# A two-layer LoRA kernel: the start in another order, B0's transposes behind the first two steps, and W1 and C' moved by tiles of columns

## The reference

```
x = x + (x W0^T + b0 + (x A0[id0]^T) B0[id0]^T)          # 32 adapters of rank 16
x = x + (x W1^T + b1 + 2 * (x A1[id1]) B1[id1])          # 32 slots of rank 16
return x
```

## Time and profile before

| | before |
|---|---|
| median of three runs | 2145.63 us |
| the profiled execution | 2145.09 us, of which the span is 2143.3 us |
| TensorE busy in matmuls | 2077.1 us (97%) |
| VectorE busy | 1594.9 us (74%) |
| ScalarE / GpSimd busy | 737.2 us (34%) / 708.3 us (33%) |
| moved by DMA | 459.08 MB, mean 214 GB/s |
| granted TensorE clock, mean of the span | 0.994 |

### The profile page before, as it was taken

One profiled execution on the slowest core, in us unless ns is written; L12 is line 12 of the kernel. 1 busy time (PEld: TensorE's weight loads), 2 busy tenths in 40 slices (PEclk: granted clock), 3 DMA queues, 4 the chain that ended last, 5 costly groups with the idle time before them and its releaser, 6 DMA issues.

```text
span 2143.3 us, 27962 instructions
## 1 busy us (share of the span) xinstructions
PE 2077.1 (97%) x9388; PEld 1715.2 (80%) x9388; DVE 1594.9 (74%) x2177; ACT 737.2 (34%) x1298; POOL 708.3 (33%) x506
## 2 busy tenths in 40 slices
PE   4999899999999999999999999999999999999999
PEld 4887687778788878888887888888888887888887
DVE  3677767967776887687877686877776886777876
ACT  4663223233322323333333333333333333333332
POOL 1133303444121545041444140544130544221443
PEclk9999999999999999999999999999999999999999
DMA  9895838796755798564798564789574688564676
GB/s 233 261 337 156 246 113 235 214 299 205 213 165 163 213 280 271 151 203 140 214 284 292 147 222 125 212 270 314 150 221 118 214 261 303 158 218 123 210 217 197
DMA packets 322298, 459.08 MB, mean 214 GB/s; under 512 B 28012, under 2 KB 135532, under 8 KB 321644
## 3 DMA queue, kind: packets, MB, share of 16 engines
q1 hardware_dynamic: 255084, 334.59, 50.9%
q10 hardware_dynamic: 67072, 122.71, 19.1%
HBM read 383.80 MB, written 74.45 MB: 214 GB/s over the span
## 4 chain that ended last, share of the span: by engine, by line
PE 76%; DVE 12%; DMA 5%; issue 3%; SPq 2%; ACT 1%; ACTq 0%; POOL 0%; DVEq 0%
PE acc L1436 22%; PE acc L1438 22%; PE acc L1437 22%; DVE w_lo L990 4%; DVE c_acc L1096 2%; PE h_acc L1366 2%; PE h_acc L1362 2%; DVE xop_lo L1015 2%; DVE c_out L1166 2%; DVE x_sum L1005 2%; PE acc L1376 1%; DMA b_raw<-pb_t 1%; DMA w_raw<-v_t 1%; PE acc L1321 1%; PE acc L1306 1%
## 5 line engine op out<-in xcount | busy, mean ns | idle before, releaser
L1436 PE MATMUL acc<-xop_hi,w_hi 128*128 128x512 f32 x2688 | 1061.0, 395 | 34.4 <-DVE w_lo L990 30.3
L791 POOL TENSOR_TENSOR w_raw<-w_raw,w_second 128x512 f32<-128x512 f32 x464 | 655.6, 1415 | 1272.0 <-DMA w_second<-wc_t 504.8
L1437 PE MATMUL acc<-xop_hi,w_lo 128*128 128x512 f32 x2688 | 1050.4, 391 | 0.0
L1438 PE MATMUL acc<-xop_lo,w_hi 128*128 128x512 f32 x2688 | 1050.1, 391 | 0.0
L990 DVE TENSOR_TENSOR w_lo<-w_raw,w_hi 128x512 fp32r<-128x512 f32 x672 | 595.9, 890 | 386.5 <-ACT w_hi L828 383.0
L828 ACT ACTIVATE w_hi<-w_raw 128x512 fp32r<-128x512 f32 x672 | 424.0, 631 | 1169.7 <-PE acc L1438 976.7
L1436 PEld LDWEIGHTS acc<-xop_hi,w_hi 128*128 128x128 f32 x2688 | 506.9, 189 | 153.5 <-DVE w_lo L990 46.9
L1438 PEld LDWEIGHTS acc<-xop_lo,w_hi 128*128 128x128 f32 x2688 | 507.1, 189 | 106.7
L1437 PEld LDWEIGHTS acc<-xop_hi,w_lo 128*128 128x128 f32 x2688 | 507.3, 189 | 101.6
L1005 DVE TENSOR_TENSOR x_sum<-x_in 128x512 f32<-128x512 f32 x240 | 222.6, 939 | 0.1
L1166 DVE TENSOR_TENSOR c_out<-acc,c_out 128x512 f32<-128x512 f32 x304 | 201.9, 681 | 7.8 <-PE acc L1376 6.2
(11 more groups left out here) (90 smaller groups left out, 890.6 us busy)
## 6 DMA issues: line engine op xcount, KB each, us to landing
w_raw<-wc_t SPq DMA_DIRECT2D x448, 256.0 KB, 3.9
w_second<-wc_t ACTq DMA_DIRECT2D x320, 256.0 KB, 4.4
w_raw<-v_t SPq DMA_DIRECT2D x208, 256.0 KB, 4.0
w_second<-v_t ACTq DMA_DIRECT2D x144, 256.0 KB, 4.4
x_in<-x_t SPq DMA_DIRECT2D x128, 256.0 KB, 6.3
out_t<-c_out SPq DMA_DIRECT2D x128, 256.0 KB, 5.3
w_part<-w_t SPq DMA_DIRECT2D x32, 512.0 KB, 6.8
x_in<-w_t SPq DMA_DIRECT2D x64, 256.0 KB, 6.1
```

The lines of the kernel that those rows point to most:

```text
L791: nc.gpsimd.tensor_tensor(w_raw[:, r, :], w_raw[:, r, :], w_second[:, n % RAW2, :], ALU.add if sign > 0 else ALU.subtract).then_inc(w_summ ...
L1436: nc.tensor.matmul(bank[:, :], wh, xh, start=(k == 0), stop=False)
L1437: nc.tensor.matmul(bank[:, :], wl, xh, start=False, stop=False)
L1438: mm = nc.tensor.matmul(bank[:, :], wh, xl, start=False, stop=end)
```

## The change

It has five parts.

1. *Layout of U.* A new view `x_pre` lies over `x_in`: tiles by column block first. A load takes 512 neighbouring floats (2 KB) of one row block for each partition and fills one column block of four moving tiles. There are still eight loads a block, of 256 KB each. Readers see a tile as 4 pieces of 128 floats, 4 KB apart.
2. *Layout of C'.* A view `c_pre` does the same for C', but for blocks 0 and 1 of pass 0. Two tiles are stored by one DMA, in rows of 1 KB: the 64 stores of 256 KB become 16 of 256 KB and 24 of 512 KB.
3. *Loads at the start.* ScalarE's queue issues A1 and SyncE's B0; before it was the other way round. Parts 4 and 5 are loaded ahead of the biases. B1's rows are loaded in the first two steps, and the store of `b0t_t` stands in step 2.
4. *Copies and splits at the start.* VectorE copies parts 0 and 1 out of PSUM. ScalarE and VectorE split the first two weights and parts 0 and 1 before they turn to U's tiles; A1 is split ahead of step 0. `h_bias` is zeroed by ScalarE.
5. *B0's transposes.* They stand behind steps 0 and 1 (`B_AFTER`), eight each, and what hangs on them one to two steps later.

The diff, cut to its core:

```diff
-    E_AFTER, Q_AFTER = 3, (5, 6)
+    B_AFTER, E_AFTER, Q_AFTER = (0, 1), 3, (5, 6)
...
+        x_pre = over("x_pre", [P, 4, TT, KH, P], fp32, "x_in")
+        c_pre = over("c_pre", [P, 4, TT, KH, P], fp32, "c_out")
...
+        def by_columns(pl, b):
+            return pl < PRE and (pl, b // 2) != (0, 0)
...
             def load_x(pl, half, th, k):
                 b = block_no(half, th)
                 if pl < PRE:
-                    sp.dma_start(as_tiles(x_in[:, b, k, :]), columns_of(w1_t, pl, th, half * KH + k)
-                                 ).then_inc(x_loaded[b], 16)
+                    o, kh = divmod(k, 2)
+                    row = (half * KH + kh * KS) * P
+                    sp.dma_start(flat(x_pre[:, b, o, kh * KS:(kh + 1) * KS, :]),
+                                 w1_t[(2 * pl + th) * TT + o, :, row:row + SW]).then_inc(x_loaded[b], 16)
...
                         if pl < PRE:
+                            if by_columns(pl, b) and m % 2 == 0:
+                                continue
...
+                            if by_columns(pl, b):
+                                src = c_pre[:, b, :, m - 1:m + 1, :].rearrange("p o m n -> p o (m n)")
+                                row -= P
...
             for b in range(BATCH):
-                sp.dma_start(a1_raw[:, b, :, :], lora_a1[...]).then_inc(a1_loaded, 16)
+                sp.dma_start(b0_rows[b * RANK:(b + 1) * RANK, :], lora_b0[...]).then_inc(b0_loaded, 16)
+            for n in PARTS_AT[-1]:
+                load_part(n + PIN)
             for l, bias_d in enumerate((bias0, bias1)):
                 sp.dma_start(bias[:, l, :], bias_d).then_inc(bias_loaded, 16)
...
+                if g < 2:
+                    for b in range(4 * g, 4 * g + 4):
+                        sp.dma_start(b1_rows[b * RANK:(b + 1) * RANK, :], lora_b1[...]).then_inc(b1_loaded, 16)
+                if g == 2:
+                    sp.wait_ge(t_copied, 4)
+                    sp.dma_start(b0t_t[:, :], flat(b0t_raw[:, :, :])).then_inc(b0t_stored, 16)
...
             # TensorE, in the loop of steps
+                    if s in B_AFTER:
+                        pe.wait_ge(b0_loaded, BATCH * 16)
+                        for n in range(2 * s, 2 * s + 2):
+                            turn(n, [b0_rows[:, (4 * n + i) * P:(4 * n + i + 1) * P] for i in range(4)])
```

More of the change, by code:

```diff
@@ L197, in parts_split @@
     def parts_split(g):
-        return [n for n in range(NPART) if PART_G_AT[n] == g + 1]
+        return [n for n in range(2, NPART) if PART_G_AT[n] == g + 1]
     def ended(n):
@@ L392, in block_no, with as_tiles, shaped, x_of @@
             return half * 2 + th
+        def as_tiles(ap):
+            return ap.rearrange("p (o n) -> p o n", o=TT)
+        def shaped(pl, ap):
+            return as_tiles(ap) if pl < PRE else ap
+        def x_of(pl, b, k):
+            return x_pre[:, b, :, k, :] if pl < PRE else x_in[:, b, k, :]
+        def by_columns(pl, b):
+            return pl < PRE and (pl, b // 2) != (0, 0)
+        def c_of(pl, b, m):
+            return c_pre[:, b, :, m, :] if by_columns(pl, b) else shaped(pl, c_out[:, b, m, :])
         def x_tile(q, which, k):
             dh, th = PRODUCTS[q % NPROD][3][which]
-            return x_in[:, block_no(dh, th), k, :]
+            return x_of(q // NPROD, block_no(dh, th), k)
+        def stores(b, pl):
+            return sum(MH // 2 if by_columns(p, b) else MH for p in range(pl))
         def wait_x(eng, q, which):
@@ L537, in load_w @@
                     for b in range(4):
-                        sp.wait_ge(out_stored[b], (PRE if i == M2 else 1) * MH * 16)
+                        sp.wait_ge(out_stored[b], stores(b, PRE if i == M2 else 1) * 16)
                 sp.wait_ge(w_lo_ready, s - RAW + 1)
@@ L657, in _ @@
             for n in PARTS_AT[-1]:
-                load_part(n + PIN)
-            for n in PARTS_AT[-1]:
                 store_part(n)
-            for b in range(BATCH):
-                sp.dma_start(b1_rows[b * RANK:(b + 1) * RANK, :],
-                             lora_b1[bass.ds(adapter_of(1, b), 1), :, :].rearrange("o r n -> (o r) n")
-                             ).then_inc(b1_loaded, 16)
-            sp.wait_ge(t_copied, 4)
-            sp.dma_start(b0t_t[:, :], flat(b0t_raw[:, :, :])).then_inc(b0t_stored, 16)
             for g in range(NG):
@@ L894, in load_second @@
                     for b in range(4):
-                        act_e.wait_ge(out_stored[b], (PRE if i == M2 else 1) * MH * 16)
+                        act_e.wait_ge(out_stored[b], stores(b, PRE if i == M2 else 1) * 16)
                 if n >= RAW2:
@@ L1189, in _ @@
                     w_split_lo(g + 2)
-                if g == 0:
-                    dve.wait_ge(a1_hi_ready, 1)
-                    nc.vector.tensor_tensor(a1_lo[:, :, :, :], a1_raw[:, :, :, :].rearrange("p b k r -> p k b r"),
-                                            f(a1_hi[:, :, :, :]), ALU.subtract).then_inc(a1_lo_ready, 1)
                 for n in parts_split(g):
                     split_part_lo(n)
-                if g == 0:
+                if g - 1 in B_AFTER:
+                    for n in range(2 * (g - 1), 2 * g):
+                        t_copy(n, flat(b0t_raw[:, 4 * n:4 * n + 4, :]))
+                if g == 2:
                     dve.wait_ge(t_copied, 4)
```

115 lines of the change are left out of this document (62 added, 53 removed).

## The result

| | before | after |
|---|---|---|
| median of five runs each, same chip | 2145.63 us (2140.78 to 2146.95) | 2128.48 us (2124.88 to 2136.15) |
| ratio, with its 95% interval | | 0.993 (0.9905 to 0.9955) |
| the profiled execution | 2145.09 us | 2124.88 us, of which the span is 2123.2 |

A forecast was written before the change was run, and what follows sets the result against it. TensorE, busy 97% of the span, was taken as the bound, gains coming only from idle time and low clock. Start 17.8, M3 6.0 and later waits 4.0 make 27.8 us off 2145.09: 2117 us, range 2105 to 2131.

The forecast's parts named there:

- two rivals (2126 and 2127): Supply gives out behind the start, 2126 us, chance 0.15; only the start's gain comes, 2127 us, chance 0.12.
- the start alone: Rival, chance 0.12: `q_half`'s round trips keep their own latency, later stalls stay, only the start's 17.8 us come: 2127 us.
- the start: Up to the small matmuls ahead of step 2: reached at 33.1 us, not 50.88; 17.8 us won, bounds 13.2 and 20.0.
- the stall in M3: M3 of pass 0: stall of 8.8 us behind U's loads shrinks; 6.0 us won, between 0 and 8.8.
- the signs that I had named for "right": Early first matmul, no `vp_lo` wait, small matmuls at full clock, U's window over 300 GB/s, short M3 wait and load issues.
- the signs for "wrong": U after 20 us, waits for parts in steps 2 to 5, 5 us wait ending M3, or VectorE lines 50 ns dearer.
- The premise of the start: In 7.5 to 20 us, U's 512-byte pieces cost about double: 174 GB/s, against 309 to 349 with longer rows.
- The second rival: Rival, chance 0.09: 512 bytes cost nothing, the queues' mix is slow; U lands at 23.2, 11.1 us won, 2134 us.
- the small matmuls: The 24 ahead of step 1 run without a wait at the high clock, 3.02 us, where they took 5.04.
- 350 to 850 us: TensorE's 16.4 us of waits in 13 places: a quarter, 4.0 us, won; between 8 won and 2 lost.
- The supply: Rival, chance 0.15: 13.1 MB in the first 44 us come late, TensorE waits in steps 2 to 5, 9 us lost: 2126.
- The pieces: Rival, chance 0.04: reading or writing in pieces slows VectorE in passes 0 and 1; at 0.3 us each, 2153 us.

The follow-up runs named there:

- E1: Changed kernel with U loaded in pieces of 512 bytes again, against the changed kernel: 2133.43 us, ratio 0.9952 to the kernel before.
- E9: Changed kernel with U's loads and C's stores as in the kernel before, so the new order alone: 2131.97 us, ratio 0.9936 to the kernel before.
- E3: Kernel before with the new layouts of U and C' and nothing else: 2141.55 us, ratio 0.9979 to the kernel before.
- E6: Changed kernel with A1 and B0 swapped back to the queues they had before: 2134.67 us in one run.
- E7: Kernel before with each load of B0's rows going to 16 partitions eight apart, not 16 neighbours: 2140.37 us, ratio 0.998 to the kernel before.
- E4: Changed kernel with B0's first eight transposes put behind the small matmuls ahead of step 1: 2126.87 us, ratio 0.9934 to the kernel before.
- E11: Changed kernel again, unedited, for a second profile: 2129.95 us, ratio 0.9931 to the kernel before.
- E2: Changed kernel with C' stored as before, 64 stores of 256 KB in pieces of 512 bytes: 2126.82 us, ratio 0.9918 to the kernel before.
- E10: Changed kernel with each load of B0's rows cut into four column pieces of 2 KB rows, still to 16 neighbouring partitions: 2133.51 us in one run.

## Why the prediction was right, and where it was not

The time, 2128.48 us, lies in the range only because two rivals (2126 and 2127) had pulled its upper end over my forecast's own range. The gain, 15 to 17 us, is a little over half of the 27.8 us that I had summed, and the nearest number on my list is that of the rival "the start alone", 2127. Its account is not what happened: the start won less than it said, and the stall in M3 did shrink. Of the signs that I had named for "right", four failed: the first 128x512 matmul starts at 19.17 (16 to 19 said), the small matmuls ahead of step 2 at 36.79 (near 33), the wait in M3 ends at 222.47 and is 3.79 us (near 215 and under 2), and SyncE takes 3.31 us for the first two of U's loads there (well under 1 us each). None of the signs for "wrong" showed in the profile after.

- **The premise of the start failed.** I wrote "So the pieces of 512 bytes cost about double". E1 and E9 move the same pieces at 318 to 320 GB/s, and E3 moves rows of 2 KB at 192. What made the window slow were B0's rows beside U: moved to ScalarE's queue again they bring 209 GB/s back (E6), spread over the partitions they let 272 through (E7). The result was on my side because the change did both things at once, which is luck. The second rival had the mechanism (the mix of the queues), and a wrong time: it let U land at 23.2 as before, though the change takes B0 out of the mix.
- The Trainium skill, page "DMA: Bandwidth & Descriptors", section "Specifications", gives 512 bytes as the least transfer for line rate. The runs agree: 318 to 320 GB/s in pieces of 512 bytes, 340 in rows of 2 KB (windows of 7.5 to 20 us, with rows of 1 KB among them). I had weighed that rule and gave it 0.09, on the ground that "the share is full and the bytes are few"; a full share says that packets are under way, not that they are short or long.
- **The start was mis-sized: 17.8 said, 14.1 measured at the place I named (50.88 minus 36.79), 13.2 kept (11.3 to 13.8 over four profiles).** The rate of U was right (340 GB/s, U at 15.87). The difference is in B0's rows again: part 2 shares its time with them and lands 1.1 us late, TensorE waits 2.2 us for them at 25.5 (I had them at 22.1, at 330 GB/s; the window moved 156), and step 0 itself takes 7.06 us in place of 6.47. That last 0.6 us is the clock: matmuls start 0.42 us or more apart for the first 5.0 us of step 0 (to 23.4), for 3.7 us in the kernel before (to 32.4), and the 1.3 us more at half the pace cost about 0.65 by estimate. That is 3.9 us; the rest of the chain up to there was 0.2 faster than I had it. Behind step 3 `make_e` waits 0.8 us for `b0t_lo`, which I had costed at nothing. In E4, without the wait for B0, TensorE waits 1.9 us for a copy of ScalarE's.
- What I said of the small matmuls was right in the first profile: no wait for `vp_lo`, a clock of 1.00, 24 in 2.95 us ahead of step 1. In E11 and E2 the clock fell there behind the wait for B0 (4.45 and 4.44 us). I had priced B0's lateness at its own length.
- **M3: 6.0 said, 3.7 in the first profile, 1.5 as the mean over the profiles.** The sum itself was off: 3.52 us and a third of the remaining 5.3 are 5.3 us, not 6.0. I had said that nearly all of the stall hangs on U's backlog, and let the matmuls at the slow clock go with it. A wait of 2.9 us or more stays in every profile, the matmuls behind it still run slowly (the first takes 0.80 us after as before), and in five kernels a second wait followed.
- **350 to 850 us: 4.0 said, nothing measured.** TensorE waits 15.9 us in 12 places there after (330 to 830) against 16.4 in 13; the 4th to 14th product took 529.6 to 538.6 us in all kernels, in no order. "A quarter" stood on no row. The waits of TensorE from 330 to 830 us:

```profile
PE acc L1474 <- DVE w_lo L1021: 15.9, 12, 3.2
```

- The supply held (in steps 2 to 5 TensorE waits for no part). The pieces cost VectorE nothing: 997 ns for `scale_c` against 987, 877 for `xop_lo` against 928, 888 for the sums against 912 and 680 for the updates against 679. The 928 holds eight instructions of pass 2 that the changed kernel has in a row of their own at 1091 ns; without them, at that price, it would be about 887. Groups by form on VectorE to 850 us, after:

```profile
L1036 DVE TENSOR_TENSOR x_sum<-x_pre 128x512 f32<-128x512 f32 x80 | 70.1, 888 | 0.1
L1129 DVE SCALAR_TENSOR_TENSOR c_acc<-x_pre,bias,c_acc 128x512 f32<-128x512 f32 x64 | 63.8, 997 | 0.1
L1199 DVE TENSOR_TENSOR c_pre<-acc,c_pre 128x512 f32<-128x512 f32 x80 | 53.1, 680 | 0.0
L1047 DVE TENSOR_TENSOR xop_lo<-x_pre,xop_hi 128x512 fp32r<-128x512 f32 x32 | 27.0, 877 | 3.4 <-ACT xop_hi L872 3.4
```

Open: which of the two terms that B0's loads leave after the spreading (502 to 583 ns for 8 KB, against 384 at the rate of W0's packets of 1 KB) is their length, their source or the small number of packets of a load. E10 didn't tell, and it wasn't tried further. Open too is what U's longer rows are worth over the whole kernel (E1, E3 and E9 above).

## What to carry to other kernels

When a window shows full DMA engines and a low rate, look at every transfer in it, not at the one you wait for: take the suspect out of the window and see whether the low rate goes with it. Look first for the same pieces in other windows of the trace that you have. A load that writes few neighbouring partitions with long rows belongs where nothing urgent moves. And price a stall by what is queued in it only if a second profile shows it at the same size: here single profiles differ by up to 4.7 us around M3 and by 8 us over passes that no edit touched. A small change to the start needs more than one profile as well: the same start won 11.3 to 13.8 us.
